# Slots in halves for the attention passes of a two-block attention kernel, and a layer norm in two separate steps

## What is computed

```python
# L0: 16 heads of 64, keys and values from the context
attn = einsum(qh * scale, kh) + side          # side: [B, 1, 512, 512]
attn = where(key_mask == 0, -1e9, attn)
x = ln(softmax(attn) @ vh @ w_o + x)
# L1: 16 heads of 32, twice, then the feed-forward layer
x = ln1(x + mha(x, x, sa..., pair_mask))
x = ln2(x + mha(x, ctx, ca...))
x = ln3(x + relu(x @ w1.T + b1) @ w2.T + b2)
```

## Time and profile before

| | us |
|---|---|
| median of 3 runs | 4583.33 |
| lowest and highest | 4579.64, 4585.48 |
| the profiled execution's own time | 4581.47 |
| its span | 4579.7 |
| PE busy | 4275.4 (93%) |
| DVE busy | 3459.9 (76%) |
| ACT busy | 2752.3 (60%) |
| POOL busy | 1486.0 (32%) |

### The profile page before, as it was taken

The page is one execution under the profiler, slowest core; times in us unless marked ns, Lnnn a source line. Parts: engine busy times, 40 slices in busy tenths (PEclk is TensorE's granted clock), DMA queues, the critical chain, the costliest instruction groups (busy, mean ns, idle before and its releaser), DMA issues. The chain is left out here.

```text
span 4579.7 us, 79492 instructions
## 1 busy us (share of the span) xinstructions
PE 4275.4 (93%) x23152; PEld 3455.4 (75%) x23152; DVE 3459.9 (76%) x7115; ACT 2752.3 (60%) x5977; POOL 1486.0 (32%) x1641
## 2 busy tenths in 40 slices
PE   8999999999999999999999988999999998999999
PEld 6887878887777777777777766777777776888887
DVE  6777777777787788888888889988888887433334
ACT  5655666655556677777777777777777776111111
POOL 2222222222223244444444444444444442100011
PEclk9999999999999999999999999999999999999999
DMA  2211112111111210000000011100011012100010
GB/s 93 72 48 48 57 60 79 58 49 48 48 59 58 67 47 29 19 24 28 28 20 23 30 59 45 38 19 28 28 37 37 24 42 81 51 32 27 34 44 33
DMA packets 108971, 200.38 MB, mean 44 GB/s; under 512 B 12208, under 2 KB 12208, under 8 KB 108720
## 3 DMA queue, kind: packets, MB, share of 16 engines
q1 hardware_dynamic: 108720, 197.73, 13.2%
HBM read 155.73 MB, written 41.94 MB: 43 GB/s over the span
## 5 line engine op out<-in xcount | busy, mean ns | idle before, releaser
L1485 POOL TENSOR_SCALAR QS<-QK 32x1024 fp32r<-32x1024 f32 (+2 forms) x1152 | 1176.2, 1021 | 1975.7 <-DVE QK L1216 1144.4
L1066 ACT ACTIVATE R<-psT 128x512 fp32r<-128x512 f32 x1536 | 916.2, 596 | 1000.7 <-PE psT L823 982.6
L1058 ACT ACTIVATE PR<-PR,MN 128x512 f32<-128x512 f32 x1536 | 1104.4, 719 | 68.8 <-DVE MN L1201 37.9
L1299 DVE TENSOR_TENSOR R<-psT,R 128x512 fp32r<-128x512 f32 x1536 | 1049.3, 683 | 20.7 <-ACT R L1066 18.5
L823 PE MATMUL psT<-ID,PR 128*128 128x128 f32 x6144 | 942.8, 276 | 81.8 <-DVE R L1299 66.3
L1201 DVE CUSTOM_DVE_ANT_0 PR<-psS,RAW 128x512 f32<-128x512 f32 x1024 | 700.7, 684 | 378.0 <-PE psS L804 281.7
L823 PEld LDWEIGHTS psT<-ID,PR 128*128 128x128 f32 x6144 | 751.1, 142 | 258.2 <-DVE R L1299 70.0
L845 PE MATMUL psV<-R 128*64 128x512 f32 (+1 forms) x3072 | 877.7, 409 | 35.6 <-DVE OG L1229 33.6
L845 PEld LDWEIGHTS psV<-R 128*64 128x64 f32 (+1 forms) x3072 | 472.1, 158 | 254.3 <-issue 38.6
L807 PE MATMUL psS<-QS 128*128 128x512 f32 x1024 | 500.2, 488 | 56.4 <-POOL QS L1485 30.7
L1075 ACT ACTIVATE PR<-psS,COLS 128x512 f32<-128x512 f32 x128 | 88.3, 690 | 555.7 <-PE psS L763 555.7
(11 more groups left out here) (117 smaller groups left out, 8002.2 us busy)
## 6 DMA issues: line engine op xcount, KB each, us to landing
x<-Y SPq DMA_DIRECT2D x96, 256.0 KB, 2.0
RAW<-x SPq DMA_DIRECT2D x96, 256.0 KB, 2.7
Y<-x SPq DMA_DIRECT2D x96, 256.0 KB, 3.6
RAW<-in_ctx_t SPq DMA_DIRECT2D x92, 256.0 KB, 2.9
RAW<-in_w SPq DMA_DIRECT2D x68, 256.0 KB, 2.7
RAW<-in_x SPq DMA_DIRECT2D x60, 256.0 KB, 3.6
RAW<-in_side SPq DMA_DIRECT2D x60, 256.0 KB, 2.6
Y<-in_x SPq DMA_DIRECT2D x32, 256.0 KB, 3.4
```

What stands on the lines that cost most here:

```text
L1058: nc.scalar.activation(prob(st, k), prob(st, k), ACT.Exp, bias=MN[:, k % 8:k % 8 + 1], scale=-1.0, accum_out=row_sums(st, SM, g)[:, qt, j: ...
L1066: nc.scalar.activation(PT[h % 2][:, 0, :, qt * P:(qt + 1) * P], turned(place[st.name][k]).rearrange("p (k t) -> p k t", k=NT), ACT.Copy).t ...
L1299: nc.vector.tensor_tensor(lo, turned(place[st.name][k]).rearrange("p (k t) -> p k t", k=NT), f32(hi), ALU.subtract).then_inc(t_evac, 1)
L1485: nc.gpsimd.tensor_scalar(to, pair, 1.0, 1.0, ALU.mult, ALU.mult).then_inc(stacked, 1)
```

## The change

The rules are replaced by two tables, `WIDE` for L0a and L0b and `NARROW` for SA and CA, in which every step of projections, splits, sums and layer norm has a slot of its own, in halves. SCORE, MAX, EXP, TURN, P_HI and P_LO keep their slots. NORM is divided into CENTRE (subtract the mean, times the gain) and NORM (times the deviation, plus the offset), each with a slot. Weights are loaded and split at other slots and partly in other buffers. The first batch of SA and the last batches of L0b and CA get mixtures of the tables. The loops of FF keep their order.

```diff
-            add(NT * h + (8, 8, 9, 9)[kt], "PV", (h, kt))
-        add(NT * h + 10, "HEAD_LO", h)
-        add(NT * h + 11, "HEAD_SUM", h)
+            add(NT * h + table["PV"][kt], "PV", (h, kt))
+        steps = ["HEAD_LO", "HEAD_SUM"]
+        for step in steps:
+            add(NT * h + table[step], step, h)
...
+WIDE = {
+    "PV": (8.5, 10, 10, 10), "HEAD_LO": 10.5, "HEAD_SUM": 11,
...
+    "STATS": (42, 43, 46.5, 48),
...
+    "CENTRE": (43, 44, 47.5, 48.5),
+    "NORM": (44.5, 45.5, 49, 49.5),
...
+NARROW = {
+    "PV": (8, 9, 10, 10), "HEAD_LO": 10.5, "HEAD_SUM": 11,
...
+        ("K", 0): ((-6, -6, -6, -6), -4, -3),
...
+        ("V", 0, 0): ((-4.5, -4, -3.5, -2.5), -2, 2.5),
...
+    "X_TURN": (-18.5, -18, -15.5, -12),
...
-                    if name == ("K", 0) and st.context:
-                        pe.wait_ge(cs_lo, tal["cs_lo"].done(tal["cs_lo"].marked(NT - 1)))
+                    if name in (("K", 0), ("V", 0, 0), ("V", 0, 1)):
+                        if st.context:
+                            pe.wait_ge(cs_lo, tal["cs_lo"].done(tal["cs_lo"].marked(NT - 1)))
+                        else:
+                            pe.wait_ge(j_evac, tal["j"].done(tal["j"].marked(("x", NT - 1))))
...
-            def normalise(tt):
-
-                n = tal["rstd"].next()
-                i = tal["gain"].next()
+            def centre(tt):
+
+                tal["gain"].next()
                 m = tal["mv"].next()
                 dve.wait_ge(mv_ready, tal["mv"].done(m))
                 nc.vector.scalar_tensor_tensor(out=Y[:, tt], in0=Y[:, tt], scalar=MV[:, tt, 0:1], in1=ROWS[:, 1],
                                                op0=ALU.subtract, op1=ALU.mult).then_inc(y_gain, 1)
+                tal["gain"].mark(tt)
+
+            def normalise(tt):
+
+                n = tal["rstd"].next()
                 dve.wait_ge(rstd, tal["rstd"].done(n))
-                dve.wait_ge(y_gain, tal["gain"].done(i))
+                dve.wait_ge(y_gain, tal["gain"].done(tal["gain"].marked(tt)))
```

More of the change, by code:

```diff
@@ L78 @@
     "VAR",
+    "CENTRE",
     "NORM",
@@ L155, in add @@
         ev.append((slot, step, what))
-    def job(name, slots, later=0):
-        for part, slot in enumerate(slots):
-            add(slot, "JOB", (name, part))
-        if name[0] != "OUT":
-            add(slots[-1] + 1 + later, "J_HI", name)
-            add(slots[-1] + 2 + later, "J_LO", name)
     for s in range(T):
@@ new lines, in timetable @@
+        for piece in range(3):
+            add(NT * h + table["STACK"][0 if h % st.per_group == 0 else 1][piece], "STACK", (h, piece))
+    for name, (parts, hi, lo) in table["JOB"].items():
+        for part, slot in enumerate(parts):
+            add(slot, "JOB", (name, part))
+        add(hi, "J_HI", name)
+        add(lo, "J_LO", name)
+    for tt in range(NT):
+        for part, slot in enumerate(table["OUT"][tt]):
+            add(slot, "JOB", (("OUT", tt), part))
+        steps = ["X_TURN", "X_HI", "X_LO", "LOAD_X", "LOAD_RES", "RES", "OUT_SUM", "NORM", "STORE"]
+        steps += ["C_HI", "C_LO", "LOAD_C"] if st.context else []
+        steps += ["STATS", "VAR", "CENTRE"] if st.norm else []
+        steps += ["LOAD_SIDE", "SIDE"] if st.bias == "side" else []
+        for step in steps:
+            add(table[step][tt], step, tt)
@@ new lines, in last_batch @@
+def last_batch(st):
+    own = timetable(st, table_of(st))
+    if st.name == "L0b":
+        shift, heads = 32, 8
+        late = {}
+        for slot, step, what in timetable(STAGES[-1], NARROW):
+            if step in ("HEAD_LO", "HEAD_SUM"):
+                what -= heads
+            elif step == "PV":
+                what = (what[0] - heads, what[1])
+            late[step, what] = slot - shift
+        by_group = ("RECIP", "SPREAD", "R_TURN", "PASS", "SCALE", "GROUP_HI", "GROUP_LO")
+        keep = lambda step, what: step in ("EXP", "TURN", "P_HI", "P_LO") or step in by_group and what < NG - 1
+        later = lambda slot, step, what: slot if slot < st.steps or keep(step, what) else max(late[step, what], st.steps)
+        return [(later(slot, step, what), step, what) for slot, step, what in own]
+    if st.name == "CA":
+        return timetable(st, {**NARROW, **{k: tuple(tuple(st.steps + s for s in v) if k == "OUT" else st.steps + v for v in row)
+                                           for k, row in FORWARD.items()}})
+    return own
@@ L256, in drain_steps @@
     st = STAGES[i]
[L257 to L258 removed]
+    return [(slot - st.steps, step, what, st, -1, B - 1) for slot, step, what in last_batch(st) if slot >= st.steps]
 def in_order(ev):
@@ L273, in first_pass @@
     st, ev = STAGES[i], []
-    for e in own_steps(st):
-        if e[4] == 1 or e[4] == 0 and not (st.name == "L0b" and e[1] in SAME):
+    for e in own_steps(st, first_batch, (0,)) + own_steps(st, offs=(1,)):
+        if e[4] == 1 or not (st.name == "L0b" and e[1] in SAME):
             ev.append(e)
```

192 lines of the change are left out of this document (103 added, 89 removed), and 22 rows, old and new, of tables (NARROW, WIDE).

## The result

The changed kernel takes 4324.25 us (median of 4 runs, 4320.36 to 4325.14) against 4582.76 us of the kernel before beside it (4 runs, 4579.64 to 4585.48): a ratio of 0.9434, 95% interval 0.9418 to 0.9451.

The account below looks back on a forecast made before the run. PE was taken as the bound, standing still some 410 us because DVE's extra work stands in heaps. 4581.5 - 164 (account) + 29 (PV) + 5 (loads) = 4451.5 us; the median lies 1.9 above, so 4453; range 4375 to 4540.

Parts of the forecast that it names:

- the account of slots: Slot-by-slot timing of PE and DVE over a pass of L0a, L0b, SA, CA: 164 us saved over eight batches.
- the term for PV in three slots: In SA and CA, shorter distances between heads' PVs make PE wait: +1.8 us per pass, +29 us in all.
- the 5 us for loads: In L0a and L0b, context tiles loaded fewer slots ahead of C_HI may come late: 0.3 us per pass, +5 us.
- the 0.8 is the one fitted number: In every attention pass, MAX starts no earlier than 0.8 us after its SCORE; this delay was fitted to the old order.
- the beginning of a batch: Ahead of SCORE 0, V jobs give PE 9.2 us of work instead of 4.9, so POOL is in time; nothing added.
- the clock's paragraph: PE at 1.2 GHz after standing still over 2 us ahead of SCORE 0; some 80 us in all, inside the fit.
- The clock stays up: Rival: with stalls short enough PE's clock no longer falls, two thirds of 80 us come on top: 4400 us, chance 0.15.
- Many short stalls bring it down more often: Rival: three more low-clock stretches per pass in SA and CA, 82 us more: 4535 us, chance 0.05.
- The wait for psV takes over: Rival: HEAD_LO and HEAD_SUM queue on ACT and DVE, PV waits, 186 us more over 16 passes: 4603 us, chance 0.09.

Follow-up runs that it names:

- the fill: Kernel before, SCORE 23 written 10 times in SA and CA, five useless matmuls into psJ behind TURN 61 in middle passes: 4570.2 us, ratio 0.9969.

## Why the prediction was wrong

The direction, the bound (PE, held up by heaps on DVE) and half of the stages were right; the size was not. Two steps failed: the account of slots gave too little for SA and CA (94 of the 129 us), and the term for PV in three slots had the wrong sign (29).

**L0a and L0b: right.** The account gave 3.0 and 6.4 us per pass; measured are 3.0 and 6.4, and the stages fell from 762.6 to 738.9 and from 807.1 to 757.1 us, 74 together where 8 x 9.4 = 75 were counted. Nothing of the 5 us for loads shows in these passes.

**PV in three slots: the wrong sign.** The prediction measured the way from PV to PV in PE work, found it shortened, and charged +29 us, with ends of 0 and 56. Taken back it costs 68.5 us, and made alone it gains 62. The distances did shrink; but the same move spreads PE's work more evenly over a head's slots, and that outweighs them. The charge was added to an account that already had the gain in it: with 0.5 us it gives 3.0 and 2.7 us per pass for this part alone, 46 of the 62. Without the charge the sum would have been 4424 us, still 100 too high. And DVE, which empties psV, comes sooner when no heap stands ahead of HEAD_SUM: the wait fell to 20.1 us.

**SA and CA: the account was mis-sized.** This is the larger miss. It gave 5.8 and 5.3 us per pass; measured are 10.8 and 12.1 (means of the six middle passes), some 94 us more over sixteen passes. With the +29 and the +5 that is 128 of the 129. The cause lies in "the 0.8 is the one fitted number". The fit took in what the account had no term for: 3.6 and 5.1 us per pass of the old order that the true delay of 0.5 leaves unexplained. The prediction noted for the clock alone that it was inside the fit "in proportion"; but these parts didn't shrink in proportion, they nearly all went. What the runs showed to be in them: the norm's pair with HEAD_SUM and so PV behind it (40 us, the account gave 10), the beginning of a batch (32 us with the projections there, where the account gave 15 and "I add nothing" stood), and the falls of the clock (13 us by the fill, for 73 of the 151 us at the lower level that went). One reading behind the clock's paragraph was off as well: ahead of SCORE 0 PE hadn't stood still for over 2 us, but for 0.55 and 1.36 us with a TURN between them, and the clock fell even so.

**What adds up.** PV 68, output and norm 51, V(0,*) with its neighbours 32, x and context 10: 161 us, taken back one at a time. Some 9 of them (PV's) lie in L0a and L0b, so 152 stand against the 188 that SA and CA gained. The remaining 36 weren't separated; Q(2) and Q(3), the other V jobs, parts that help each other, and the clock are in them.

**The rivals.** "The clock stays up" named the right state (0.997 over the run, 1.00 in CA's passes) at too high a price, 53 us: the fill's 13 us for 73 us of low clock would make 27 for the 151 that went, an estimate that takes the filler for free. And 4400 would still have been too slow. "Many short stalls bring it down more often" didn't come: PE's waits of over 0.15 us fell from 309 to 177, and the clock fell six times in place of 47. What the section of the page "TensorE: Matmul & The Clock Gate" of the Trainium skill that the prediction weighed tells of another kernel didn't happen here. "The wait for psV takes over", the one that ended slower, is refuted by its own row, 20.1 us where it needed over 200.

## What to carry to other kernels

When a slot model has a fitted constant, read the constant from the trace first (a start to a start where both engines are free) and look at what the model then leaves unexplained: here the remainder of the old order was the part of the gain that the forecast missed. Before charging an edit for shortened distances, ask what it does to the evenness of the bottleneck engine's work, and test the part alone in the kernel before; a move that looks like a cost was the largest gain. On an in-order engine, count what stands behind a burst (here the readout of psV), not only the burst. And in a kernel with loops, read the branch rows of every run beside its waits: here a turn that grew from 0.2 to 3.8 us hid behind a wait that was put down to POOL, and it spoiled an experiment on something else.

## What was not expected of the hardware

**DVE and POOL hold each other up.** The norm's two instructions and the splits of context read two operands from SBUF. Durations in ns, least, median, longest, in the changed kernel:

```profile
L1269 DVE SCALAR_TENSOR_TENSOR Y<-Y,MV,ROWS x128: 717/746/1600, 905.7 to 4314.4; 128x512 f32<-128x512 f32 x128
...
L1247 DVE TENSOR_TENSOR R<-RAW,R x92: 678/896/1524, 12.8 to 3432.2; 128x512 fp32r<-128x512 f32 x92
...
L1388 DVE TENSOR_TENSOR R<-psT,R x1536: 635/685/693, 46.3 to 3586.4; 128x512 fp32r<-128x512 f32 x192
```

The third reads one operand from psT; it is never over 0.69 us in 1536 times, with POOL at work beside it in many. The first takes at most 0.75 us in the 70 cases where POOL is idle; of the 58 that overlap with POOL 49 are no longer either, and nine are, up to 1.60 beside a STACK piece. POOL is held up too: STACK pieces of 1.04 us take 1.25 and 1.40 beside the pair's instructions. The Trainium skill, page "SBUF — State Buffer", section "SBUF: two separate sides", has the rule: DVE, with two inputs from SBUF, and GpSimd share one pair of ports, and whoever comes first keeps it for its whole instruction. The trace agrees in that only instructions with two operands from SBUF are stretched. Who came first it doesn't settle: the longest began 0.02 us ahead of its STACK piece and waited all the same. The prediction priced these instructions at 0.60 to 0.73 us wherever they stood; in a timetable, the places of STACK and of the norm belong together.

**A turn of the loop isn't free.** ACT stood 1.26 us at it in CA, and 1.59 with a body twice as long, though its instructions' operands were ready; PE's branch took 0.2 us in some loops and 3.3 to 5.3 in others. The Trainium skill, page "Advanced Engine Details and Errata", section "Control Flow Timing", gives branches of some 50 to 110 ns. The branch rows of ACT and DVE agree (0.04 and 0.07 us), but the engines stand far longer than their branch takes, and PE's longest is some fifty times the page's figure. In L0a and L0b of the changed kernel the turn costs nothing because it is short there, 0.24 to 0.37 us on ACT and DVE and 0.2 on PE.
